# A two-layer graph network: block messages as two float32r parts, and destination one-hots written as float32r

## The reference

```python
def _L1_gnn_ref(x, edge_index, edge_type, edge_emb_W, msg_W, msg_b, upd_W, upd_b, ln_g, ln_b):
    et = edge_emb_W[edge_type]
    m_in = jnp.concatenate([x[src], et], axis=-1)
    m = jax.nn.relu(m_in @ msg_W.T + msg_b)
    agg = jax.ops.segment_sum(m, dst, num_segments=x.shape[0])
    deg = jax.ops.segment_sum(jnp.ones_like(dst, dtype=x.dtype), dst, num_segments=x.shape[0])
    agg = agg / jnp.clip(deg, 1.0)[:, None]
    out = agg @ upd_W.T + upd_b
    h = x + out
    ...
x = x + _L0_gnn_ref(h, edge_index, ...)
h = jnp.maximum(_layernorm(x, axis=-1), 0.0)
x = x + _L1_gnn_ref(h, edge_index, edge_type_16, ...)
```

## Time and profile before

| | |
|---|---|
| time, median of 3 runs | 1657.06 us (1656.15 to 1657.53) |
| profiled execution, first to last instruction (its span) | 1654.6 us |
| busy over the span: PE, PEld | 1510.1 us (91%), 1258.9 us (76%) |
| busy over the span: DVE | 1213.1 us (73%) |
| busy over the span: ACT | 509.0 us (31%) |
| busy over the span: POOL | 1176.4 us (71%) |
| mean granted clock of TensorE | 0.976 |

### The profile page before, as it was taken

How to read it: one execution, slowest core, us unless ns; L and a number is a source line. 1 busy time by engine, 2 the same in 40 slices (tenths; PEclk the granted TensorE clock), 3 DMA queues, 4 the chain that set the end, 5 groups by cost and what they waited for, 6 DMA issues and landing times.

```text
span 1654.6 us, 37443 instructions
## 1 busy us (share of the span) xinstructions
PE 1510.1 (91%) x14439; PEld 1258.9 (76%) x14439; DVE 1213.1 (73%) x2964; ACT 509.0 (31%) x742; POOL 1176.4 (71%) x1169
## 2 busy tenths in 40 slices
PE   0289999999999997899999997799999999999995
PEld 0278889889889884455555556799989899999994
DVE  6899999999999863113234233687888888898886
ACT  5434444444444442001012111322222222232222
POOL 3787777787776627777777775577777777777772
PEclk9989999999999998999999998799999999999998
DMA  5444555554554546988888887556665666665662
GB/s 144 129 146 153 170 172 165 178 173 157 172 176 160 177 140 208 299 242 246 269 236 277 264 260 239 182 164 193 187 177 170 170 184 194 186 190 164 191 180 58
DMA packets 179051, 312.07 MB, mean 189 GB/s; under 512 B 28610, under 2 KB 123412, under 8 KB 178868
## 3 DMA queue, kind: packets, MB, share of 16 engines
q1 hardware_dynamic: 137908, 225.63, 41.7%
q0 software_dynamic: 40960, 83.95, 19.4%
HBM read 228.36 MB, written 81.09 MB: 187 GB/s over the span
## 4 chain that ended last, share of the span: by engine, by line
PE 50%; DVE 17%; POOL 17%; issue 9%; DMA 3%; DVEq 1%; ACT 1%; SPq 0%; POOLq 0%; ACTq 0%
PE banks L1258 50%; POOL rows L923 16%; DVE region_b L1740 3%; DVE region_a L1740 2%; DMA rows<-table,src_all 1%; DVE src_hot L1740 1%; DVE hot L1740 1%; DMA region_a<-near_tab 1%; DVE src_in_all L1740 1%; DVE region_b L1772 1%; DVEq L2242 1%; DVE stats L1638 1%; DVE region_b L1765 1%; DMA x_or_cnt<-in_x 0%; DVE region_a L1780 0%
## 5 line engine op out<-in xcount | busy, mean ns | idle before, releaser
L923 POOL DMA_INDIRECT rows<-table,src_all x992 | 1095.1, 1104 | 374.9 <-issue 310.3
L1258 PE MATMUL banks<-region_a,htab 128*128 128x256 bf16 (+1 forms) x4128 | 639.2, 306 | 6.9 <-issue 4.1
L1258 PEld LDWEIGHTS banks<-region_a,htab 128*128 128x128 bf16 (+1 forms) x4128 | 405.7, 99 | 174.4 <-issue 11.3
L1258 PE MATMUL banks<-region_a 128*128 128x256 f32 (+1 forms) x1896 | 331.0, 322 | 0.0
L1210 ACT ACTIVATE region_a<-banks 128x1024 bf16<-128x1024 f32 (+2 forms) x272 | 234.9, 864 | 302.6 <-PE banks L1258 302.6
L1258 PEld LDWEIGHTS banks<-region_a 128*128 128x128 f32 (+1 forms) x1896 | 264.0, 161 | 33.3 <-issue 3.6
L2250 DVE TENSOR_TENSOR agg<-agg,banks 128x128 f32 (+1 forms) x171 | 54.4, 318 | 262.9 <-PE banks L1258 195.5
L1258 PEld LDWEIGHTS banks<-hot,rows 128*128 128x128 bf16 (+1 forms) x2560 | 204.6, 129 | 24.5 <-issue 16.6
L1258 PE MATMUL banks<-hot,rows 128*128 128x128 bf16 (+1 forms) x2560 | 212.3, 239 | 11.8 <-DMA rows<-table,src_all 10.2
L2307 DVE TENSOR_SCALAR region_a<-columns,slot_dst 128x256 f32<-128x256 f32 x676 | 211.4, 379 | 0.0
L1258 PE MATMUL banks<-type_rows,region_b 128*128 128x128 bf16 x1092 | 179.5, 221 | 1.3 <-DVE region_b L2166 1.3
(11 more groups left out here) (222 smaller groups left out, 1494.2 us busy)
## 6 DMA issues: line engine op xcount, KB each, us to landing
region_a<-near_tab SPq DMA_DIRECT2D x100, 384.0 KB, 4.4
near_tab<-region_a SPq DMA_DIRECT2D x68, 448.0 KB, 3.0
region_b<-in_etype SPq DMA_DIRECT2D x52, 512.0 KB, 5.5
near_tab<-region_a SPq DMA_DIRECT2D x68, 384.0 KB, 2.5
region_a<-near_tab SPq DMA_DIRECT2D x32, 512.0 KB, 5.4
rows<-table,src_all POOLq DMA_INDIRECT x992
src_in_all<-src_tab SPq DMA_DIRECT2D x52, 224.0 KB
region_b<-type_tab SPq DMA_DIRECT2D x52, 224.0 KB
```

Source lines behind the costliest of these rows:

```text
L923: nc.gpsimd.indirect_dma_start(out=to[:, c, :], out_offset=None, in_=tab[layer], in_offset=bass.IndirectOffsetOnAxis(ap=cols[:, c:c + 1], ...
L1258: return nc.tensor.matmul(to, left, right, start=start, stop=stop)
```

## The change

Only the third pass is changed, and there only the blocks.

- ScalarE writes the ReLU as float32r (`message_top`), a 4-byte type with fewer digits; it rounds.
- VectorE computes what the rounding left, `max(message_ps, 0) - message_top`, as float32r too (`message_rest`), one instruction for each unit (`message_rests_of`). It needs `message_ps` still in place, so the picks of unit u now wait for `message_rests` of unit u-2.
- The destination one-hots are written as float32r by the same instructions (`dst_wide`).
- `slot_sum` is two float32r products, one with each part, where there was one float32 product.
- `dst_all` and the two `rows` buffers change their places in SBUF to make room; the second `message_rest` lies behind the group rows.

```diff
-        rows = [sb(f"rows{s}", [P, C, K3 * F], bf16) for s in range(2)]
-        rows_f = [r[:, :, :].rearrange("p c f -> p (c f)")[:, 0:2 * GE].bitcast(fp32).rearrange("p (c f) -> p c f", f=F)
-                  for r in rows]
+        rows_all = sb("rows_all", [P, 2 * C * K3 * F], bf16)
+        rows = [rows_all[:, s * C * K3 * F:(s + 1) * C * K3 * F].rearrange("p (c f) -> p c f", f=K3 * F) for s in range(2)]
+        rows_f = [rows_all[:, 2 * s * GE:2 * (s + 1) * GE].bitcast(fp32).rearrange("p (c f) -> p c f", f=F) for s in range(2)]
...
-        dst_hot_f = [take([P, J, WIN_B]) for _ in range(2)]
-        messages = [take([P, J, F]) for _ in range(2)]
+        WIDE, MESSAGES = 4 * J * WIN_B, 4 * J * F
+        dst_wide = [placed(f"dst_wide{k}", [P, J, WIN_B], fp32r, "region_a", k * WIDE) for k in range(2)]
+        message_top = [placed(f"message_top{k}", [P, J, F], fp32r, "region_a", 2 * WIDE + k * MESSAGES) for k in range(2)]
+        message_rest = [placed("message_rest0", [P, J, F], fp32r, "region_a", 2 * WIDE + 2 * MESSAGES),
+                        placed("message_rest1", [P, J, F], fp32r, "rows_all", 8 * GE)]
+        assert 2 * WIDE + 3 * MESSAGES <= 4 * 6300 and 8 * GE + MESSAGES <= 4 * C * K3 * F
...
-                        nc.scalar.activation(messages[u % 2][:, 0:m, :], message_ps[u % 2][:, 0:m, :], ACT.Relu)\
+                        nc.scalar.activation(message_top[u % 2][:, 0:m, :], message_ps[u % 2][:, 0:m, :], ACT.Relu)\
...
             def slot_sum(u, j):
 
                 t = UNITS[u][j]
-                return mm(bsum_ps[2][0], messages[u % 2][:, j, :], dst_hot_f[u % 2][:, j, :], t == 0, t == BUCKETS - 1)
+                mm(bsum_ps[2][0], message_top[u % 2][:, j, :], dst_wide[u % 2][:, j, :], t == 0, False)
+                return mm(bsum_ps[2][0], message_rest[u % 2][:, j, :], dst_wide[u % 2][:, j, :], False, t == BUCKETS - 1)
...
-                            pe.wait_ge(messages_ready, c.unit(u - 2, since=2))
+                            pe.wait_ge(message_rests, c.unit(u - 2, since=2))
                         for j in range(len(UNITS[u])):
                             last = pick(c, u, j)
                         last.then_inc(unit_picked, 1)
                     if u > 0:
-                        pe.wait_ge(messages_ready, c.unit(u - 1, since=2))
+                        pe.wait_ge(message_rests, c.unit(u - 1, since=2))
...
                     def destination_hot(u):
                         dve.wait_ge(unit_summed, c.unit(u - 2))
                         for j, t in enumerate(UNITS[u]):
-                            last = V.tensor_scalar(dst_hot_f[u % 2][:, j, :], columns1[:, :],
+                            last = V.tensor_scalar(dst_wide[u % 2][:, j, :], columns1[:, :],
                                                    slot_dst[:, b * BUCKETS + t:b * BUCKETS + t + 1], None, ALU.is_equal)
                         last.then_inc(dst_hot_ready, 1)
+
+                    def message_rests_of(u):
+                        m = len(UNITS[u])
+                        dve.wait_ge(messages_ready, c.unit(u, since=2))
+                        V.scalar_tensor_tensor(out=message_rest[u % 2][:, 0:m, :], in0=message_ps[u % 2][:, 0:m, :], scalar=0.0,
+                                               in1=message_top[u % 2][:, 0:m, :].bitcast(fp32), op0=ALU.max, op1=ALU.subtract)\
+                            .then_inc(message_rests, 1)
...
                         if hot_next is not None:
                             group_hot(hot_next)
                         if layer == 2:
+                            if u > 0:
+                                message_rests_of(u - 1)
                             destination_hot(u)
...
                             early_last(at)
+                    if layer == 2:
+                        message_rests_of(U - 1)
```

More of the change, by code:

```diff
@@ L40, in gnn_program @@
     bf16 = mybir.dt.bfloat16
+    fp32r = mybir.dt.float32r
     i32 = mybir.dt.int32
@@ L94, in gnn_program, with placed @@
     with ctx:
+        begins = {}
         def sb(name, shape, dt=fp32):
+            begins[name] = -(-nc.sbuf_base // 32) * 32
             return ctx.enter_context(nc.sbuf_tensor(name, shape, dt))
+        def placed(name, shape, dt, within, at):
+            return nc.alloc_sbuf_tensor_at(name, shape, dt, offset=begins[within] + at)
         def sem(name):
@@ L117, in gnn_program @@
         src_all = sb("src_all", [P, GROUPS * C], i32)
-        dst_all = sb("dst_all", [P, GROUPS * C], i32)
         base_all = sb("base_all", [P, GROUPS], i32)
@@ L121, in gnn_program @@
         far = sb("far", [P, GROUPS * C])
+        dst_all = sb("dst_all", [P, GROUPS * C], i32)
         tile_no = sb("tile_no", [P, BLOCK_COLS, 2], fp16)
@@ L234, in gnn_program @@
         near_in = [take([P, 2 * len(PAIR_UNITS[0]) * WIN_B], bf16, 2) for _ in range(RING)]
-        take = carver(region_a)
-        dst_hot_f = [take([P, J, WIN_B]) for _ in range(2)]
-        messages = [take([P, J, F]) for _ in range(2)]
+        WIDE, MESSAGES = 4 * J * WIN_B, 4 * J * F
[4 more added lines that the diff above has]
+        assert 2 * WIDE + 3 * MESSAGES <= 4 * 6300 and 8 * GE + MESSAGES <= 4 * C * K3 * F
         take = carver(region_a)
@@ L342, in gnn_program @@
         messages_ready = sem("messages_ready")
+        message_rests = sem("message_rests")
         in_tile_ready = sem("in_tile_ready")
```

## The result

The changed kernel takes 1713.78 us (median of four runs, 1712.7 to 1717.63), the kernel before 1657.3 us beside it (four runs, 1656.15 to 1658.35). The ratio is 1.0345, its 95% interval 1.0327 to 1.0363: slower, as predicted, 13 us above the predicted 1701 and inside the range. The profiled execution took 1714.22 us, with a span of 1712.5.

A forecast was written before the change was run, and what follows sets the result against it. TensorE, POOL and VectorE were taken as nearly balanced, with VectorE becoming the bound: 600.1 + 6.1 + 8 + 7 = 621.2 us for the third pass, 43.7 more than 577.5, so 1701 us; range 1675 to 1755.

The forecast's parts named there:

- the bound named: Third pass: VectorE becomes the bound, needing 600.1 us where the stage had 577.5, so TensorE's saving is given back.
- VectorE's busy time in the pass: Third pass: 104 new VectorE instructions at a marginal 1.006 us each add 104.6 us to 495.5.
- L2359 waits for the gather: VectorE's addition of gathered group rows, third pass: 6.1 us of waits at the start, 7 us later.
- L2359 waits for TensorE: VectorE's addition of gathered group rows, third pass: its wait for TensorE shrinks from 45.4 to 8 us.
- The surcharge of 65 ns: New VectorE instruction: scalar_tensor_tensor form costs 65 ns over a plain addition, giving 1153 and 1018 ns.
- The wait for the types: Ahead of the group-row addition: type rows behind the slot sums cost VectorE 0.2 us in 39 groups, 8 us.
- rival C: TensorE's clock falls in the third pass; half its work at 1.2 GHz needs 643 us: 1723 us, chance 0.06.
- the main case: Third pass: VectorE as the bound, whole kernel at 1679 to 1729 us, chance 0.70.
- A: Destination one-hots as float32r lose VectorE's fast rate, 131 ns more each, 88 us in all: 1789 us, chance 0.10.
- B: Slot sums: a float32r product isn't one pass, 0.221 us each, waits 58 instead of 8 us: 1751 us, chance 0.06.
- D: New VectorE instruction reads two elements a step, adding 0.5 us each; deciding marginal cost 0.59 us: 1650 us, chance 0.05.
- E: New VectorE instruction's marginal cost lies near 0.59 us, so no change: 1657 us, chance 0.03.

## Why the prediction was right, and where its sizes were off

The predicted span was 43.7 us above that of before, the measured one is 57.9 above. By the profile the bound named was the right one, and it came about in the way described: VectorE's work fills the pass, and what TensorE saves is given back. That the number came as near as 13 us is in part luck: the waits for TensorE were 32 us too low, and the added work and the gather 17 us too high.

| term of the sum | predicted, us | measured, us |
|---|---|---|
| VectorE's busy time in the pass | +104.6 | 587.4 - 495.5 = +91.9 |
| L2359 waits for the gather | 6.1 + 7 | 8.4 |
| L2359 waits for TensorE | 8 | 40.3 |
| other idle time of VectorE | 0 | 51.3 - 48.7 = 2.6 |
| length of the pass | +43.7 | +61.2 |
| behind the pass | about 0 | -3.2 |

- **The new instruction**: 1081 and 948 ns, not 1153 and 1018. The surcharge of 65 ns, taken from L1945, isn't there; without it my own 1088 and 953 ns come within 1%. The shorter instruction makes 7.4 of the 12.7 us by which the term was too high; 3.6 more are the destination one-hots, 207.8 us in all against 211.4. L1945 takes its scalar from a tile and L2327 has a constant, which may be the reason; no run separates them. The Trainium skill ("VectorE: DVE Perf Modes", the errata section) states (N + 151) / 0.96 ns for a float32 two-tensor addition; taken as an estimate for this instruction it is 1091 and 958 ns, and this trace agrees within 1.1%.
- **The wait for the types**: the step that failed. I priced it at 0.2 us in 39 groups. In the 26 ordinary ones it is 0.68 in the mean, from three things in the chain of 2.55 us: the hand-overs (0.06 and 0.10), the first product's extra 0.11, and a pace of 0.118 where I used 0.110. And in one of the three steps of a block, u = 4, VectorE has six one-hots (1.80 us behind the new instruction) beside the sums of seven slots, where I had put like against like. The rows of the changed order, an even step with a 128x896 rest and six one-hots, showed that pairing. It adds only a little: the ordinary waits are 0.77 us in the mean there, against 0.62 with seven and seven and 0.64 with six and six. These 26 make 17.8 us. The 13 late ones make the other 22.5.
- **The clock**: I had it at 1.00 in the forecast and at 22 us in rival C, worked out as if TensorE became the bound. It fell to 0.93 in the mean, and the loss came another way: stretches at half clock make TensorE start the chain late, and VectorE, which is the bound, waits. The timelines show it for the group at 1165.35; in the same window ahead of all 13 late groups the mean clock was 0.59 to 0.76, while of the 26 ordinary ones 18 had 1.00 and 8 had 0.76. No group with 1.00 in that window was late, and the blocks' second groups, compared with each other, show the same: four had 1.00 and waited 0.53 to 0.70 us, nine had less and waited 0.74 to 2.52. That goes together; holding the clock up, which would prove it, wasn't tried. So the time came out of the main case with a part of C in it.
- **Rivals A and B** are refuted: one-hots at a median of 343 ns against 341, products 0.118 us apart against 0.221 for a float32 instruction. D fell with what the new instructions added, 91.9 / 104 = 0.88 us each against a deciding point of 0.59, and E with it.
- **The gather** mostly hid, as argued. **Behind the pass** 3.2 us were won that I had not counted; TensorE is busy 5.84 us there and was 7.7 before, the rest I have not traced.
- My own tests, "over 95% busy" and "wrong if VectorE keeps idle time of over 40 us or the clock leaves 1.00", came out as 92%, 51.3 us and 0.93. By these signs I was wrong in part, and they point at the two things missing: the loop of waits through both engines (VectorE waits for type rows that wait for VectorE's own instruction) and the clock.

What the experiments add is a limit. The split of the 61.2 us into 92 of work and 31 of idle time won back is arithmetic on the profile of the first comparison, exact for an engine that works in order, but no run under its condition took one part away. In the traces of the experiments VectorE, with the new instruction, is busy only 514 to 556 of 730 us, its added work costs no time that can be seen, and the loss of 1% may be the new wait. That VectorE's work is what costs in the first comparison, and that the type rows ahead of the slot sums would win something there, stays read from the profile. Why the experiments' chips run this program 400 us slower is open.

## What to carry to other kernels

- Moving work from the busiest engine to the next wins nothing if the next has less slack than the work moved: here VectorE's 82 us of idle time against 92, and of the 82 a part is waiting that doesn't go away. Count the slack of the receiver first, then the chain that the new producer sits in.
- When a cheaper stage hangs on a new producer, write its chain out end to end, with both hand-overs and the real pairing of sizes (seven slots against six); 0.5 us in each of 39 places are some 20 us.
- An engine that gets idle time can also get a lower clock, as here: 0.99 at 99% busy, 0.93 at 77%. Its saving has to be taken at the clock of after, and what it does behind an idle stretch can take longer (0.213 us a product against 0.118).

## What the runs showed of the hardware

- A float32r product of a 128x128 and a 128x256 operand costs 0.118 us in a row (0.213 at the lower clock), against two times 0.221 for a float32 one. VectorE writes float32r at its old one-operand rate: 343 against 341 ns for 256 elements.
- TensorE's clock dropped for some 20 short stretches of the pass while the engine was busy 77% of it; in the case shown it had stood still for 4.43 us.
- The same program took 1657 us in the first comparison and 2053 to 2061 on the three chips of the experiments. There TensorE often stands still without waiting for anything that the profile shows (104.6 us of "issue" above, 14.7 us in the third pass of the first comparison). Two such gaps on TensorE's timeline of the changed kernel on chip 6:

```profile
1566.93 0.33 PE L1270 MATMUL banks<-htab,src_hot 128*128 x3 [1.14 <-issue]
...
1568.35 0.22 PE L1270 MATMUL banks<-type_rows,region_b 128*128 128x128 bf16 x1 [1.09 <-issue]
```
